# Attention outputs of a chunked recurrence: state rows and early v rows joined in one product, with a score buffer for each chunk

## The chip, the cores and the metric

One core of one Trainium2 chip. The metric is the device time of the program in microseconds, the median of the runs. The engines are named as the profile names them: PE is TensorE, DVE VectorE, ACT ScalarE, POOL GpSimd, and SP SyncE, which here only begins transfers.

## What is computed

The input x has 4 sequences of 1024 rows of 1024 numbers. Each row is normalised. From it come q, k and v (weights rounded to -1, 0 and 1 times a scale), 16 heads of 64, and a gate from a second linear layer. The attention is a recurrence over chunks of T = 128 rows, with a decay s for each head:

```python
def step(S, qkv_c):
    qi, ki, vi = qkv_c
    scores = jnp.einsum('bhtd,bhsd,hts->bhts', qi, ki, mask)     # mask: exp(-s (t - s')) for t >= s', else 0
    intra = jnp.einsum('bhts,bhsd->bhtd', scores, vi)
    cross = jnp.einsum('bhtd,ht,bhde->bhte', qi, lam_t, S)
    o = scale * (intra + cross)
    kv = jnp.einsum('bhtd,ht,bhte->bhde', ki, lam_rev, vi)
    return (lam_T * S + kv, o)
```

The outputs are normalised twice, projected, multiplied by the silu of the gate, and added to x.

## The kernel before

The rows are cut into 16 blocks (i = 0 to 15) of two chunks (c = 0 and 1), so 32 chunks g = 2i + c; eight chunks make a sequence, and the first chunk of one (g = 0, 8, 16, 24) has no state to read. Everything is held with channels on the partitions, two heads (e = 0, 1) of 64 on the 128 partitions of a pair r, eight pairs. Large products (q and k, v, the gate, the projection) run in float16 pieces against rounded weights; from block 2 on, v and the gate use seven products p1 to p7 of quarter size (Strassen's scheme), k from block 3 (`BY_TOKENS`) and the projection from block 4 to 14 (`BY_PRODUCTS`). Their sums of quarters are made by DVE.

There is no scheduler: each engine runs one written-out list of instructions in order, and semaphores hold them to each other. What matters around the change, in the order of a block:

- PE: q, the k products, projection products of the block before, the v products, then for chunk 0 the scores, v product p4, a gate product, a turn of k, the outputs (`outputs`, L938 and L942), the state update (L919); then the same for chunk 1 with gate products between. k product p4 (L839) waits for DVE's `add_k(i, 1)` (L1407), v product p4 (L813) for `add_v(i, 1)` (L1399).
- `outputs`: for each pair r, two f32 products state x decayed q (128 columns, L938) and two products v x masked scores (L942) into the same PSUM. The state of a pair is a 128 x 128 block whose off-diagonal quarters are zero.
- DVE: sums of quarters (L1378 and others), centring of the next block's rows (L1333, L1335), `decay_k_tokens` (L1532), `add_v`, `mask_scores` (L1523: scores in PSUM times the mask), `weight_o`, `add_state` (L1567).
- POOL: `add_out` (L2532), `norm_scale`, `decay_q` (L2481: q times its decay, two halves of 128 x 512 for a chunk), `decay_state` (L2493, two of 64 x 512), `bias_z` (L2466, L2468), `sum_squares`, `output_scale` (L2521, L2525), and in blocks 1 to 4 sums of weights. `decay_q(i, 0)` stands after `norm_scale(i + 1, ...)`; `decay_q(i, 1)` stands in `attention(i, 0)` after `bias_z`, since there is one buffer of decayed q, free after the outputs of chunk 0.
- SP: loads of x, stores of the output, and the turn of the row statistics through memory, in a written order.
- Masked scores and decayed q have one buffer each, in the tile `arena`; `scores_m` is shared in memory with `b_turned`, and with the row and pieces of the projection products.

Of the kernel before, what the change touches and what calls it, by code (L numbers as in the profile page):

```python
# [36 lines left out]
def program(nc, x, qkv_w, proj_w, decay, ffn_w, ffn_b, norm_cols, x_turned, out):  # L37
# [17 lines left out]
    with ExitStack() as ctx:  # L55
# [34 lines left out]
        QL_OFF = V_OFF + CHUNKS * C  # L90
        ST_OFF = QL_OFF + 2 * C
        SM_OFF = ST_OFF + 2 * PR * P
        ARENA = SM_OFF + H * T
# [4 lines left out]
        with nc.sbuf_tensor("arena", [P, ARENA], F32) as arena:  # L98
            pass
        sb("arena_low", [P, SM_OFF])  # L100

        o_row = sb("o_row", [P, CPH, T])
        o_split = sb("o_parts", [P, 3, 2, CPH, T], F16)
# [26 lines left out]
        v_tok = arena[:, V_OFF:QL_OFF].rearrange("p (c n) -> p c n", c=CHUNKS)  # L130
        q_decay = arena[:, QL_OFF:QL_OFF + C].rearrange("p (r t) -> p r t", r=PR)
        k_decay = arena[:, QL_OFF + C:QL_OFF + 2 * C]

        ow_first = k_decay.rearrange("p (r t) -> p r t", r=PR)
        state = arena[:, ST_OFF:SM_OFF].rearrange("p (k r e) -> p k r e", k=2, r=PR)
        scores_m = arena[:, SM_OFF:ARENA].rearrange("p (h e r t) -> p h e r t", h=HALF, e=2, r=CPH)

        b_turned = arena[:, SM_OFF:ARENA].rearrange("p (c j t) -> p c j t", c=CHUNKS, j=NCB)
# [7 lines left out]
        lam_T = sb("lam_T", [P, PR])  # L146
# [13 lines left out]
        diag = sb("diag", [P, CHUNKS, T])  # L160

# [36 lines left out]
        s_state0 = sem("state_zeroed")  # L198
# [138 lines left out]

        def passes_on(g):

            return g - g // NCHUNK  # L340
# [5 lines left out]
        def of_half(i, c, h):  # L346
            return chunk(i, c) * HALF + h + 1

# [347 lines left out]
        def tensor_program(pe):  # L696
# [514 lines left out]
        def vector_program(dve):  # L1211
# [297 lines left out]
            def mask_scores(i, c):  # L1509
# [8 lines left out]
                for half in range(HALF):  # L1518
                    dve.wait_ge(s_sc, HALF * g + half + 1)
                    if g > 0:  # L1520
                        dve.wait_ge(s_o, HALF * (g - 1) + half + 1)
# [1273 lines left out]
```

## Time and profile before

| | before |
|---|---|
| median of 3 runs (lowest to highest) | 1314.8 us (1313.32 to 1315.18) |
| span of the profiled execution | 1314.2 us |
| PE busy | 1289.1 us, 98% |
| DVE busy | 1008.4 us, 77% |
| ACT busy | 617.4 us, 47% |
| POOL busy | 600.4 us, 46% |
| granted TensorE clock | full in all 40 slices |
| moved by DMA | 90.3 MB, 69 GB/s over the span |

The profiled execution lasted 1314.2 us from its first to its last instruction, 0.6 us under the median of the timed runs. The page's busy times are averages over all stages; where a stage is bound by the hand-over from one engine to another is seen in the timelines of that stage. In a timeline, the columns are the start, the length (both in us), the engine, the line, the operation, the output and inputs, the shapes and the count of merged instructions, and in brackets the idle time before with what ended it. The length of several merged instructions runs from the start of the first to the end of the last; consecutive DVE instructions overlap by some 0.08 us.

### The profile page before, as it was taken

How to read it: one execution, taken by the hardware profiler on the slowest of the kernel's cores; microseconds unless marked ns; L12 is line 12 of the kernel's file. 1: busy time of each engine (PE TensorE's matmuls, PEld its weight loads, DVE VectorE, ACT ScalarE, POOL GpSimd, SP SyncE). 2: the span in 40 equal slices, each digit the busy share in tenths (PEclk: the TensorE clock that was granted, in tenths of full speed). 3: DMA queues.
4: the chain of work that ended last, by engine and by line, in shares of the span. 5: the costliest groups of instructions: out<-in, count | busy, mean ns of one | idle time of the engine just before them, and what ended most of it. 6: DMA issues, size and time to landing. Idle time of an engine off the chain costs nothing.

```text
span 1314.2 us, 25908 instructions
## 1 busy us (share of the span) xinstructions
PE 1289.1 (98%) x10263; PEld 824.8 (63%) x10263; DVE 1008.4 (77%) x1567; ACT 617.4 (47%) x1216; POOL 600.4 (46%) x537
## 2 busy tenths in 40 slices
PE   4999999999999999999999999999999999999998
PEld 2577767675665757566574656657566575756655
DVE  7888367687676887878788787877878788787755
ACT  5884144344434635446354544644436363544621
POOL 1442785955354435354432535435333443535352
PEclk9999999999999999999999999999999999999999
DMA  9631101203012030210303011030300304021020
GB/s 361 248 97 66 57 34 37 101 33 106 1 38 100 17 121 18 76 46 18 121 17 120 18 57 65 17 121 18 94 28 19 119 17 121 17 58 49 1 65 32
DMA packets 33433, 90.32 MB, mean 69 GB/s; under 512 B 10529, under 2 KB 10785, under 8 KB 33314
## 3 DMA queue, kind: packets, MB, share of 16 engines
q1 hardware_dynamic: 33024, 88.65, 20.0%
q8 instruction: 82, 1.34, 0.4%
q14 instruction: 37, 0.30, 0.1%
q10 hardware_dynamic: 290, 0.02, 0.0%
HBM read 71.85 MB, written 16.81 MB: 67 GB/s over the span
## 4 chain that ended last, share of the span: by engine, by line
PE 94%; DVE 2%; ACT 2%; DMA 1%; issue 1%; SPq 0%; POOL 0%; DVEq 0%; ACTq 0%; POOLq 0%
PE ring L854 20%; PE ring L787 13%; PE ring L813 13%; PE ring L839 12%; PE ring L1012 10%; PE ring L988 5%; PE att_ps L892 4%; PE att_ps L942 4%; PE att_ps L938 4%; PE ring L904 2%; PE att_ps L919 2%; PE ring L867 1%; PE ring L754 1%; DMA raw<-in_ffn_w 1%; ACT junk L1951 1%
## 5 line engine op out<-in xcount | busy, mean ns | idle before, releaser
L854 PE MATMUL ring<-b_lo,qkv_q 128*128 128x256 f16 x1216 | 268.2, 272 | 0.0
L854 PE MATMUL ring<-b_hi,qkv_q 128*128 128x256 f16 x1216 | 268.2, 273 | 0.0
L2532 POOL TENSOR_TENSOR xt<-xt,gate_even 128x512 f32<-128x512 f32 x58 | 90.6, 1564 | 172.5 <-DVE gate_even L1626 131.8
L854 PEld LDWEIGHTS ring<-b_hi,qkv_q 128*128 128x128 fp8e4 x1216 | 120.2, 99 | 15.8 <-issue 0.4
L854 PEld LDWEIGHTS ring<-b_lo,qkv_q 128*128 128x128 fp8e4 x1216 | 118.9, 98 | 15.6
L2506 POOL TENSOR_TENSOR sq<-sq,cols 128x1024 f32<-128x1024 f32 x29 | 55.0, 1896 | 126.8 <-DVE b_lo L1423 118.6
L2094 ACT ACTIVATE gate_even<-gate_even 128x512 f32<-128x512 f32 x60 | 37.3, 625 | 136.2 <-DVE gate_even L1454 136.1
L942 PE MATMUL att_ps<-arena 128*64 128x128 f32 x1024 | 95.0, 273 | 0.0
L938 PE MATMUL att_ps<-arena 128*64 128x128 f32 x896 | 88.5, 276 | 0.0
L1523 DVE TENSOR_TENSOR arena<-att_ps,mask 128x512 f32<-128x512 f32 x128 | 79.3, 680 | 11.0 <-PE att_ps L892 11.0
L2385 POOL TENSOR_TENSOR ln<-ln,small 128x3 f32<-128x3 f32 x32 | 37.4, 1168 | 100.2 <-DVE ln L1311 99.3
L2481 POOL TENSOR_TENSOR arena<-arena,lam_q 128x512 f32<-128x512 f32 x56 | 77.2, 1398 | 9.7 <-ACT arena L2110 7.0
L1454 DVE SCALAR_TENSOR_TENSOR gate_even<-ring,ln,gate_even 128x512 f32<-128x512 f32 x70 | 52.4, 748 | 29.0 <-PE ring L787 29.0
L2466 POOL TENSOR_TENSOR gate_even<-gate_even,bias 128x512 f32<-128x512 f32 x14 | 19.8, 1415 | 114.0 <-ACT gate_even L2070 113.9
L2110 ACT ACTIVATE arena<-ring,wscale 128x512 f32<-128x512 f32 x64 | 43.4, 679 | 58.0 <-PE ring L854 58.0
L892 PEld LDWEIGHTS att_ps<-arena 64*128 64x128 f32 x1024 | 59.7, 188 | 13.8 <-issue 13.8
L2493 POOL TENSOR_TENSOR arena<-arena,lam_T 64x512 f32<-64x512 f32 x48 | 61.6, 1283 | 13.5 <-DVE arena L1565 10.8
L892 PE MATMUL att_ps<-arena 64*128 64x128 f32 x1024 | 65.8, 278 | 0.5 <-ACT sq L2136 0.5
L1648 DVE SCALAR_TENSOR_TENSOR gate_even<-ring,wscale,gate_even 128x512 f32<-128x512 f32 x36 | 27.0, 749 | 50.7 <-PE ring L1012 36.2
L942 PEld LDWEIGHTS att_ps<-arena 128*64 128x64 f32 x1024 | 63.5, 137 | 0.7 <-issue 0.7
L2521 POOL TENSOR_TENSOR small<-small 128x1 f32<-128x1 f32 x32 | 18.5, 580 | 99.5 <-DVE small L1633 99.5
L787 PE MATMUL ring<-ffn_q,a_lo 128*128 128x512 fp8e4 x168 | 63.6, 379 | 0.0
(298 smaller groups left out, 3523.1 us busy)
## 6 DMA issues: line engine op xcount, KB each, us to landing
xt<-in_x SPq DMA_DIRECT2D x60, 512.0 KB, 3.7
out<-xt SPq DMA_DIRECT2D x31, 512.0 KB, 2.7
raw<-in_qkv_w SPq DMA_DIRECT2D x24, 512.0 KB, 15.8
y<-in_x_turned SPq DMA_DIRECT2D x14, 512.0 KB, 5.9
y_odd<-in_x_turned SPq DMA_DIRECT2D x14, 512.0 KB, 6.7
raw<-in_ffn_w SPq DMA_DIRECT2D x8, 512.0 KB, 9.8
norm_rows<-norm_out SPq DMA_DIRECT2D x14, 256.0 KB, 6.0
raw<-in_proj_w SPq DMA_DIRECT2D x6, 512.0 KB, 4.7
```

The lines of the kernel that those rows point to most:

```text
L787: ins = pe.matmul(ring[:, b, :], of[:, j, :], weights_of(weights)[:, j, :], start=(begins and j == 0 and k == 0), stop=(j == CPH - 1 and k ...
L813: ins = pe.matmul(ring[:, b, :], of[:, j, :], v_weights_of(weights)[:, j, :], start=(name in ("p1", "p5") and j == 0 and k == 0), stop=(j ...
L839: ins = pe.matmul(ring[:, b, :], of[:, j, :], k_weights_of(weights)[:, j, :], start=(name in ("p1", "p5") and j == 0 and k == 0), stop=(j ...
L854: ins = pe.matmul(ring[:, b, e * BT:(e + 1) * BT], qkv_q[:, cb, o:o + P], part[:, cb, :], start=(cb == 0 and part is b_hi and (e == 0 or i ...
L892: ins = pe.matmul(att_ps[:, 2 * half + e, j, :], k_t[rows, r, ts], q_t[rows, r, ts], start=True, stop=True)
L938: pe.matmul(att_ps[e * D:(e + 1) * D, half, j, :], state[:, passes_on(g) % 2, r, e * D:(e + 1) * D], q_decay[:, r, :], start=True, stop=Fa ...
L942: ins = pe.matmul(att_ps[e * D:(e + 1) * D, half, j, :], v_tok[:, c, r * P + e * D:r * P + (e + 1) * D], scores_m[:, half, e, j, :], start ...
L988: ins = pe.matmul(ring[:, b, :], part[:, cb, :], proj_q[:, cb, cs], start=(cb == 0 and k == 0), stop=(cb == NCB - 1 and k == 1))
L1012: ins = pe.matmul(ring[:, b, :], of[:, j, :], proj_weights_of(weights)[:, j, :], start=(name in ("p1", "p5") and j == 0 and k == 0), stop= ...
L1523: dve.tensor_tensor(scores_m[:, half, e, :, :], att_ps[:, 2 * half + e, :, :], mask[:, e, half * CPH:(half + 1) * CPH, :], ALU.mult).then_ ...
L2481: pool.tensor_tensor(q_decay[:, hs, :], q_t[:, hs, c * T:(c + 1) * T], lam_q[:, hs, :], ALU.mult).then_inc(s_ql, 1)
L2532: pool.tensor_tensor(o, o, gate_of(i)[:, c, cs], ALU.add).then_inc(s_add, 1)
```

## The change

For a non-first chunk, the first 64 tokens of the chunk (its keys) have scores with all 128 queries, the last 64 keys only with the last 64 queries, because of causality. The change uses that. For each chunk parity c there is a buffer `stacks[c]` with three sections of 64 query columns: section 0 holds (rows 0 to 63) the masked scores of the early keys with the early queries and (rows 64 to 127) decayed q of the early queries; section 2 holds zeros and decayed q of the late queries; section 1 holds the masked scores of all 128 keys with the late queries. `v_state` holds, for each head, 64 rows of v of the early keys above the 64 rows of the state. One joined product of v_state with sections 0 and 2 (128 columns) and one of v with section 1 (64 columns) replace two of 128 columns.

- `outputs`: the above; in first chunks one product of 128 columns as before. The waits for decayed q (both halves), the state, the copy of v and the zeros all stand ahead of half 0.
- `mask_scores`: four operations of 512 elements as before, cut by query half instead of head; it waits for the outputs of the same chunk a block ago.
- `decay_q`: two operations of 64 x 1024, one for each head half, from rows 0 to 63 or 64 to 127 to rows 64 to 127. `decay_q(i, 1)` moves from the middle of `attention(i, 0)` to right after `decay_q(i, 0)` (blocks 1 to 4) or after the last `add_out` of the block before (from block 5), ahead of `decay_state(i, 0)`; in block 0 it stays.
- `decay_state`: one operation of 64 x 1024. `add_state` writes both heads to rows 64 to 127.
- `copy_v`: the 64 early rows of v (256 KB) are copied by DMA into v_state; begun by SP at the end of each block's list for both chunks, by ACT for chunk 1 of block 0.
- `b_turned` moves so that it shares memory with the odd stack; some waits move with it. The host reserves less room for dynamic DMA.

```diff
@@ outputs
-                if not is_first(g):
-                    pe.wait_ge(s_ql, HALF * takes_over(g) + half + 1)
-                    if half == 0:
-                        pe.wait_ge(s_st, 2 * passes_on(g))
+                if not is_first(g) and half == 0:
+                    pe.wait_ge(s_ql, 2 * takes_over(g) + 2)
+                    pe.wait_ge(s_st, 2 * passes_on(g))
+                    pe.wait_ge(s_vcopy[c], copied(i, c))
+                    if takes_over(g) == 0:
+                        pe.wait_ge(s_zeros, CHUNKS)
...
                 for j in range(CPH):
                     r = half * CPH + j
-                    if not is_first(g):
+                    to = [att_ps[e * D:(e + 1) * D, half, j, :].rearrange("p (s t) -> p s t", s=2) for e in range(2)]
+                    v = [v_tok[:, c, r * P + e * D:r * P + (e + 1) * D] for e in range(2)]
+                    if is_first(g):
                         for e in range(2):
-                            pe.matmul(att_ps[e * D:(e + 1) * D, half, j, :],
-                                      state[:, passes_on(g) % 2, r, e * D:(e + 1) * D], q_decay[:, r, :],
-                                      start=True, stop=False, skip_group_check=True)
+                            ins = pe.matmul(to[e], v[e], stacks[c][:, 0:2, e, r, :], start=True, stop=True)
+                        continue
+
                     for e in range(2):
-                        ins = pe.matmul(att_ps[e * D:(e + 1) * D, half, j, :],
-                                        v_tok[:, c, r * P + e * D:r * P + (e + 1) * D],
-                                        scores_m[:, half, e, j, :], start=is_first(g), stop=True,
-                                        skip_group_check=True)
+                        pe.matmul(to[e], joined(g)[:, r, e, :], stacks[c][:, 0:3:2, e, r, :],
+                                  start=True, stop=False, skip_group_check=True)
+                    for e in range(2):
+                        ins = pe.matmul(to[e][:, 1, :], v[e], stacks[c][:, 1, e, r, :],
+                                        start=False, stop=True, skip_group_check=True)
@@ mask_scores
-                    if g > 0:
-                        dve.wait_ge(s_o, HALF * (g - 1) + half + 1)
-                    for e in range(2):
-                        dve.tensor_tensor(scores_m[:, half, e, :, :], att_ps[:, 2 * half + e, :, :],
-                                          mask[:, e, half * CPH:(half + 1) * CPH, :], ALU.mult).then_inc(s_scm, 1)
+                    if i > 0:
+                        dve.wait_ge(s_o, of_half(i - 1, c, half))
+                    for s, rows in enumerate((early, slice(0, P))):
+                        ts = slice(s * D, (s + 1) * D)
+                        dve.tensor_tensor(stacks[c][rows, s, :, hs, :], att_ps[rows, 2 * half:2 * half + 2, :, ts],
+                                          mask[rows, :, hs, ts], ALU.mult).then_inc(s_scm, 1)
@@ decay_q
-                pool.tensor_tensor(q_decay[:, hs, :], q_t[:, hs, c * T:(c + 1) * T], lam_q[:, hs, :],
-                                   ALU.mult).then_inc(s_ql, 1)
+                if i > 0:
+                    pool.wait_ge(s_o, of_half(i - 1, c, 1))
...
+                if c == 1 and i > 0 and by_products(i - 1):
+                    pool.wait_ge(s_ops, of_o_product(i - 1, "p3"))
+
+                    pool.wait_ge(s_add, of_out(i - 1, 0, 1))
...
+                for e in range(2):
+                    rows = slice(e * D, (e + 1) * D)
+                    q, by = (of.rearrange("p r (s t) -> p r s t", s=2)
+                             for of in (q_t[rows, :, c * T:(c + 1) * T], lam_q[rows, :, :]))
+                    pool.tensor_tensor(stacks[c][D:P, 0:3:2, e, :, :].rearrange("p s r t -> p r s t"), q, by, ALU.mult).then_inc(s_ql, 1)
+                    pool.wait_ge(s_ql, 2 * takes_over(g) + e + 1)
@@ decay_state
-                for e in range(2):
-                    rows, cs = slice(e * D, (e + 1) * D), slice(e * D, (e + 1) * D)
-                    pool.tensor_tensor(state[rows, (n + 1) % 2, :, cs], state[rows, n % 2, :, cs],
-                                       lam_T[rows, :].unsqueeze(2).to_broadcast([D, PR, D]), ALU.mult).then_inc(s_sd, 1)
-
-                    pool.wait_ge(s_sd, 2 * (n - g // NCHUNK - 1) + e + 1)
...
+                pool.tensor_tensor(to, of, lam_T[D:P, :].unsqueeze(2).to_broadcast([D, H, D]),
+                                   ALU.mult).then_inc(s_sd, 1)
@@ attention (POOL), c == 0
-                    decay_q(i, 1, 0)
-                    decay_q(i, 1, 1)
+                    if i == 0:
+                        decay_q(0, 1)
@@ the loop over blocks (POOL)
                     if by_products(i - 1):
-                        decay_q(i, 0, 0)
-                        decay_q(i, 0, 1)
+                        decay_q(i, 0)
                         add_out(i - 1, 1, 1)
                         add_out(i - 1, 1, 0)
                         add_out(i - 1, 0, 1)
+                        decay_q(i, 1)
...
-                        decay_q(i, 0, 0)
-                        decay_q(i, 0, 1)
+                        decay_q(i, 0)
+                        decay_q(i, 1)
@@ sync_program
+            def copy_v(i, c):
+
+                g = chunk(i, c)
+                if is_first(g):
+                    return
+                for by in v_at(i, c):
+                    sync.wait_ge(*by)
+                sync.wait_ge(s_o, HALF * (g - 1))
+                sync.dma_start(joined(g)[0:D, :, :, :].rearrange("p r e d -> p (r e d)"),
+                              v_tok[0:D, c, :]).then_inc(s_vcopy[c], DMA)
...
+                copy_v(i, 0)
+                copy_v(i, 1)
```

## Rows read from the trace of the kernel before

**Rows 1.** The page: the chain that ended last, share of the span by engine.
```profile
PE 94%; DVE 2%; ACT 2%; DMA 1%; issue 1%; SPq 0%; POOL 0%; DVEq 0%; ACTq 0%; POOLq 0%
```

**Rows 2.** Waits of PE: who for whom, us in total, times, longest us.
```profile
PE ring L813 <- DVE arena L1399: 1.6, 5, 0.3
```

**Rows 3.** Timeline of PE, block 9: outputs of chunk 0, state update, next product.
```profile
803.08 0.44 PE L938 MATMUL att_ps<-arena 128*64 128x128 f32 x4
...
806.63 1.10 PE L919 MATMUL att_ps<-arena,gate_odd 128*64 128x64 f32 x32
807.66 0.39 PE L787 MATMUL ring<-ffn_sum,sum_hi 128*128 128x512 fp8e4 x1
```

**Rows 4.** POOL's groups by line and shape: busy us, mean ns | idle before.
```profile
L2506 POOL TENSOR_TENSOR sq<-sq,cols 128x1024 f32<-128x1024 f32 x29 | 55.0, 1896 | 126.8 <-DVE b_lo L1423 118.6 <-ACT sq L2136 8.2
...
L2510 POOL TENSOR_TENSOR sq<-sq 128x512 f32<-128x512 f32 x29 | 36.8, 1271 | 2.3
L2510 POOL TENSOR_TENSOR sq<-sq 128x256 f32<-128x256 f32 x29 | 21.1, 729 | 2.3
```

**Rows 5.** Timeline of POOL, block 1: decay_state right after the outputs' scale.
```profile
189.50 2.15 POOL L2493 TENSOR_TENSOR arena<-arena,lam_T 64x512 f32<-64x512 f32 x2
```

**Rows 6.** Timeline, block 9: DVE's sums of quarters and POOL's decay_q beside them.
```profile
771.12 0.69 DVE L1378 TENSOR_TENSOR y_odd<-y_odd 128x512 f32<-128x512 f32 x1
...
771.82 1.26 POOL L2481 TENSOR_TENSOR arena<-arena,lam_q 128x512 f32<-128x512 f32 x1
...
771.85 1.78 DVE L1378 TENSOR_TENSOR y_odd<-y,y_odd 128x512 f32<-128x512 f32 x1
```

**Rows 7.** Timeline of DVE, block 9: the masks of chunk 1.
```profile
812.43 2.48 DVE L1523 TENSOR_TENSOR arena<-att_ps,mask 128x512 f32<-128x512 f32 x4 [0.35 <-PE att_ps L892]
```

**Rows 8.** Timeline, block 9: add_k(9, 1), k product p4, DVE's next wait.
```profile
780.51 0.74 DVE L1407 SCALAR_TENSOR_TENSOR gate_odd<-ring,wscale,gate_odd 128x512 f32<-128x512 f32 x1
...
781.85 0.38 PE L839 MATMUL ring<-k_sum_last,b_hi 128*128 128x512 fp8e4 x1
...
785.50 0.75 DVE L1648 SCALAR_TENSOR_TENSOR gate_even<-ring,wscale,gate_even 128x512 f32<-128x512 f32 x1 [2.87 <-PE ring L1012]
```

**Rows 9.** Timeline: decay_state to v product p4 in block 9; p4 in block 14.
```profile
793.25 3.48 POOL L2493 TENSOR_TENSOR arena<-arena,lam_T 64x512 f32<-64x512 f32 x2
...
794.30 2.98 DVE L1532 TENSOR_TENSOR gate_odd<-gate_odd,lam_k 128x512 f32<-128x512 f32 x2
...
797.20 1.40 DVE L1399 SCALAR_TENSOR_TENSOR arena<-ring,wscale,arena 128x512 f32<-128x512 f32 x2
...
798.65 0.39 PE L813 MATMUL ring<-v_sum_last,b_hi 128*128 128x512 fp8e4 x1
...
1190.43 0.39 PE L813 MATMUL ring<-v_sum_last,b_hi 128*128 128x512 fp8e4 x1 [0.33 <-DVE arena L1399]
```

**Rows 10.** Timeline, block 8: the second add_v and v product p4.
```profile
719.89 0.75 DVE L1399 SCALAR_TENSOR_TENSOR arena<-ring,wscale,arena 128x512 f32<-128x512 f32 x1 [0.39 <-PE ring L813]
...
721.77 0.39 PE L813 MATMUL ring<-v_sum_last,b_hi 128*128 128x512 fp8e4 x1
```

**Rows 11.** Timeline of PE, block 3: v product p4.
```profile
329.90 0.39 PE L813 MATMUL ring<-v_sum_last,b_hi 128*128 128x512 fp8e4 x1
```

**Rows 12.** Timeline of PE, block 1: the spread of the outputs' scale.
```profile
190.03 0.38 PE L973 MATMUL ring<-diag,mean_sq 128*128 128x128 f32 x1
```

**Rows 13.** Timeline, block 0: the masks of chunk 0, and its outputs.
```profile
98.81 2.47 DVE L1523 TENSOR_TENSOR arena<-att_ps,mask 128x512 f32<-128x512 f32 x4
...
100.41 0.76 PE L942 MATMUL att_ps<-arena 128*64 128x128 f32 x9
```

**Rows 14.** SP's last load in block 9 (timeline); DMA issues: count, KB, us to landing.
```profile
796.06 0.33 SPq L2673 DMA_DIRECT2D xt<-in_x  x1
...
out<-xt SPq DMA_DIRECT2D x1, 256.0 KB, 2.0
...
norm_rows<-norm_out SPq DMA_DIRECT2D x14, 256.0 KB, 6.0
```

More of the change, by code:

```diff
@@ L97, in program @@
             pass
[L98 to L103, printed above, removed]
+        arena = sb("arena", [P, ARENA])
         SQ = 2 * PR * T
@@ L197, in program @@
         s_ident, s_iota, s_cut = sem("ident_made"), sem("iotas_made"), sem("mask_cut")
-        s_state0 = sem("state_zeroed")
+        s_zeros = sem("stack_zeros_set")
+        s_vcopy = [sem(f"v_copied{c}") for c in range(CHUNKS)]
         s_ones, s_peak = sem("constants_set"), sem("peak_taken")
@@ L336, in is_last, with decays @@
             return g % NCHUNK == NCHUNK - 1
+        def decays(g):
+            return sum(not is_first(k) and not is_last(k) for k in range(g + 1))
         def passes_on(g):
@@ L347, in of_half, with copied, joined @@
             return chunk(i, c) * HALF + h + 1
+        def copied(i, c):
+            return DMA * sum(not is_first(chunk(k, c)) for k in range(i + 1))
+        def joined(g):
+            return v_state[:, passes_on(g) % 2, :, :, :]
         def of_ffn(i, c, h):
@@ L1559, in add_state @@
                 else:
-                    dve.wait_ge(s_sd, 2 * (passes_on(g) - (g // NCHUNK + 1)) + 2)
+                    dve.wait_ge(s_sd, decays(g))
                 for e in range(2):
-                    rows, cs = slice(e * D, (e + 1) * D), slice(e * D, (e + 1) * D)
-                    to = state[rows, (n + 1) % 2, :, cs]
+                    rows = slice(e * D, (e + 1) * D)
+                    to = v_state[D:P, (n + 1) % 2, :, e, :]
                     if is_first(g):
@@ L2468, in bias_z, with decay_q @@
                 pool.tensor_tensor(gate[:, 1, 0:BANK], gate[:, 1, 0:BANK], bias[:, 0:BANK], ALU.add).then_inc(s_zbias, 1)
-            def decay_q(i, c, half):
+            def decay_q(i, c):
                 g = chunk(i, c)
@@ L2490, in decay_state @@
                 pool.wait_ge(s_o, HALF * g)
-                for e in range(2):
-                    rows, cs = slice(e * D, (e + 1) * D), slice(e * D, (e + 1) * D)
-                    pool.tensor_tensor(state[rows, (n + 1) % 2, :, cs], state[rows, n % 2, :, cs],
-                                       lam_T[rows, :].unsqueeze(2).to_broadcast([D, PR, D]), ALU.mult).then_inc(s_sd, 1)
-                    pool.wait_ge(s_sd, 2 * (n - g // NCHUNK - 1) + e + 1)
+                if c == 1 and (by_products(i) or i == 1):
+                    pool.wait_ge(s_gamma, chunk(i, 0) + 1)
+                elif c == 1 and i > 1:
+                    pool.wait_ge(s_red, sums(chunk(i, 0)))
+                to, of = (v_state[D:P, k % 2, :, :, :].rearrange("p r e d -> p (r e) d") for k in (n + 1, n))
+                pool.tensor_tensor(to, of, lam_T[D:P, :].unsqueeze(2).to_broadcast([D, H, D]),
+                                   ALU.mult).then_inc(s_sd, 1)
+                pool.wait_ge(s_sd, decays(g))
             def sum_squares(i, c):
@@ L2605, in gpsimd_program @@
             pool.wait_ge(s_wout, w_n["qkv", QKV_TILES - 1])
-            pool.memset(state, 0.0).then_inc(s_state0, 1)
+            for stack in stacks:
+                pool.memset(stack[0:D, 2, :, :, :], 0.0).then_inc(s_zeros, 1)
             for i in range(NB):
@@ L2685, in load_turned, with copy_v @@
                 sync.dma_start(to, x_turned[row:row + P, :]).then_inc(s_xt[c], DMA)
+            def copy_v(i, c):
+                g = chunk(i, c)
+                if is_first(g):
+                    return
+                for by in v_at(i, c):
+                    sync.wait_ge(*by)
+                sync.wait_ge(s_o, HALF * (g - 1))
+                sync.dma_start(joined(g)[0:D, :, :, :].rearrange("p r e d -> p (r e d)"),
+                              v_tok[0:D, c, :]).then_inc(s_vcopy[c], DMA)
             def spread_norm(i):
```

65 lines of the change are left out of this document (44 added, 21 removed).

## Prediction

> **What bounds the kernel.** I read the page first: of the chain of work that ended last, 94% is TensorE (PE), in a span of 1314.2 us [rows 1]. PE is therefore the path: less PE work shortens the kernel, and any moment in which PE waits lengthens it. The second view is who waits for whom: PE waited for VectorE (DVE) in one place worth naming, the product at L813 behind the addition at L1399, five times and 1.6 us in all [rows 2]. The third is the timelines of PE, DVE and POOL in block 9, a typical one of the 16 blocks of 78.8 us. They show how much room stands between DVE and PE at the two places where DVE hands over work last. The granted clock is full throughout, so it is no term.
>
> **What PE saves.** In block 9 the outputs of chunk 0 start at 803.08 and the state update at 806.63, so the 64 instructions of the outputs (each f32 matmul is two) take 3.55 us, in groups of four 0.218 us apart, or 54.6 ns each. The update's 32 instructions have 64 columns and start at 806.63; the next product starts at 807.66. That is 1.03 us, of it some 0.15 the hand-over, so 28 ns each, or 32 with it [rows 3]. The change leaves 32 instructions of 128 columns (the joined products) and makes 32 of 64 columns: 32 x 54.6 + 32 x 28 = 2.64 us against 3.5, a gain of 0.86 us (0.72 at 32 ns). Outputs of the four first chunks keep their 128 columns. 28 chunks x 0.86 = 24 us; the bound below is 20.
>
> The Trainium skill (TensorE: Matmul & The Clock Gate, LDWEIGHTS) prices a weight load by its columns at P/1.2 ns, which as an estimate is 53 ns for 64 columns. If that set the pace, the short products would be no cheaper and the 24 us would be zero. The trace differs: such loads and matmuls follow each other in 28 to 32 ns [rows 3].
>
> **What POOL pays.** decay_q was two multiplications of 512 elements a partition and becomes two of 1024 on 64 partitions: the moves to other partitions are made half by half, and each half covers all eight pairs. POOL's time goes by elements a partition, not by partitions: two full f32 inputs cost 729 ns at 256 and 1271 at 512, a slope of 2.12 ns and so 2.35 us at 1024. With a broadcast input 1024 cost 1.90 us, and decay_state's 64 x 512 cost 1.03 undisturbed (2.15 for two, with the wait between them) [rows 4, 5]. I take 2.35 for the new operation, since both its inputs are full, with 1.9 as the bound below; nothing bounds it well above (the output goes to other partitions, in runs of 64), so 3.0 is my allowance. decay_state turns from 2 x 1.03 into one of 1.9: no term.
>
> By the Trainium skill (GPSIMD Engine Reference, Elementwise — side-by-side cycle accounting) 2048 elements take 4497 ns, so an estimate for 1024 is 2.25; every blocked operation below would be 0.1 us shorter and the sum some 3 us lower.
>
> **Why DVE pays for it too.** At 771.82 decay_q's first half starts, and DVE's subtraction of two SBUF tiles, 30 ns later, takes 1.78 us; the same operation without POOL beside it takes 0.69 [rows 6]. The DVE operation doesn't share, it runs when the POOL operation is over. Masking, which reads PSUM and one SBUF tile, is not held: four in 2.48 us while POOL sums squares [rows 7]. So masks (same count and elements), add_v and add_state keep their times, while sums, centring and decay_k_tokens stand behind POOL. What counts is the length of each POOL operation and what DVE owes PE afterwards.
>
> **Place A, the k products.** decay_q(i, 0) stays where it was, and each half holds DVE 2.35 - 1.27 = 1.08 us longer, 2.16 in all. DVE has no pause until add_k(i, 1) ends at 781.25; k product p4 waits for it and starts at 781.85 [rows 8]. A hand-over costs 0.06, so 0.54 is room. PE loses 2.16 - 0.54 = 1.6 us. DVE then waits for PE (2.87 us at 785.50 [rows 8]), so nothing is carried on.
>
> **Place B, the v products.** decay_q(i, 1), which stood behind the outputs of chunk 0 at 806.7, moves to before decay_state(i, 0), that is to 793.3. In the kernel before, the two halves of decay_state alternate there with the two decay_k_tokens of DVE (2.98 us for two that take 1.28 alone), then add_v twice, and v product p4 starts 0.06 us after them [rows 9]: no room. Now two operations of 2.35 stand in the place of two of 1.03: 2 x 1.32 = 2.6 us that PE waits. decay_state comes after them, at 799.5 to 801.4, before add_state at 807.8, and meets only masks. The wait for the last add_out is for POOL's own previous work; queued behind decay_q(i, 1) are decay_state and bias_z, whose input comes at 803.9: covered.
>
> A and B cost 4.3 us in blocks 5, 6, 7, 9, 10, 11, 13 and 14 (all eight have the same distances as block 9; of the last, block 14, the wait of p4 stands in [rows 9]): 34 us. Blocks 8 and 12 begin a sequence: no decay_q(i, 0), and no POOL work at B. There two operations come new, 4.7 less 0.2 by which the first runs under the centring; of these 4.5 us, add_v's pause of 0.39 and a room of 1.07 before p4 take 1.5 [rows 10]: 3.0 us each, 6.1.
>
> **The early blocks.** Block 3: a sum of weights on POOL has only one chunk's decays ahead of it, and p4 starts at 329.90 [rows 11]. From 316.7, the second half's start, POOL and DVE would alternate through three halves (7.05), decay_state (1.9), the sum (3.8) and DVE's four centrings (1.12 each), two decays (0.6) and two add_v (0.7): p4 at 336.2 to 336.5, and PE loses 6.3. Block 1: POOL's queue is full until it makes the outputs' scale, which is ready just ahead of decay_state at 189.50 and which PE takes at 190.03 [rows 5, 12]; four decays of +1.08 less 0.2 put it at 193.5, when PE, 1.3 us ahead, is ready at 188.8: 4.8. Block 0: the masks follow the rounding of weights without a pause and the second ends 0.3 before the outputs at 100.41 [rows 13]; decay_q, ahead of them, holds DVE 2.16 longer: 1.9. Blocks 4 and 15: 0.9 together (in 15 POOL has one sum of 3.83 already in that place).
>
> **The copies of v.** SyncE's last load of the block goes out at 796.06; v of chunk 0 is whole at 797.9, the outputs follow at 803.08, some 5 us, which B's stall doesn't shorten. A store of 256 KB lands in 2.0 us, norm_rows of the same size in 6.0 [rows 14]. I take 2.0 to 3, since the copy has 64 rows of 4 KB: hidden. At 6 it would cost 1 us in 12 blocks. Chunk 1's has 15 us of cover. After the two waits SyncE's next work is a load at the next block's start, so nothing queued behind them is late. PE's gathered waits (both halves of decay_q, the zeros, the copy) cost nothing by the same rows.
>
> **The sum.** -24 + 34.4 + 6.1 + 6.3 + 4.8 + 1.9 + 0.9 = +30.4 us. From the span of 1314.2 that is 1344.6; the measured median lies 0.6 above the span, so **1345 us**.
>
> **Rivals.**
> 1. *The operation is short* (1.9 us, as with a broadcast). A 0.7 and B 1.7 in eight blocks make 20; blocks 8 and 12, 4.2; the early ones 9: +9 net, 1324. For it: the linear rule is an extrapolation. Against: two slopes at 2.1.
> 2. *Faster: DVE isn't what PE waits for.* If at A and B DVE's operations win the port before the second halves, or the halves fall into pauses, only one of four delays remains; the stalls are under 20 us and PE's 24 decide: about 1300, at best 1291. It decides from an average delay of under 2 us a block. Against: at both places DVE has no pause and the trace alternates strictly.
> 3. *The operation is slow* (3.0 us, for the shifted partitions). Each delay grows by 0.65, A and B to 6.9: +61 us, 1376.
> 4. *The short products aren't shorter*: no 24 us, 1369. [rows 3] speak against it.
> 5. *The copy is late* (6 us or more behind other transfers): 12 us or more on top, 1357.
>
> **How the numbers follow.** The forecast has 0.60, rival 1 0.13, rival 2 0.13, rival 3 0.08, rivals 4 and 5 together 0.06. About 0.2% is what a measurement can tell from no change. Faster is 0.12 from rival 2; same 0.03 from its edge and that of rival 1; slower 0.85. The range, 1318 to 1364, reaches from under rival 1 to the forecast with operations of 2.7 us and leaves out most of rivals 2 and 3.
>
> **What would show it.** POOL's decay_q halves at 2.3 us; DVE's subtractions behind them at 2.8; decay_k_tokens two in 5.6; PE with new waits at L839 and L813 (k and v product p4) behind DVE of 1.6 and 2.6 us in each block, which the kernel before lacks; the outputs of a chunk in 2.7 us; no wait of PE for a DMA. I am wrong if PE's waits behind DVE add up to under 24 us, or if decay_q takes under 1.7.

## The result and the profile after

The changed kernel takes 1362.5 us (median of 4 runs, 1361.6 to 1362.9) against 1314.9 for the kernel before (1313.3 to 1315.2): ratio 1.0366, 95% interval 1.0351 to 1.0380. It is slower, by 47.6 us where 30 were forecast. The profiled execution spans 1361.5 us. Its page, with the columns of the page of before, has these lines: busy time by engine, the shares of the chain that ended last, and three groups of instructions.

```profile
PE 1286.5 (94%) x10263; PEld 807.4 (59%) x10263; DVE 1072.9 (79%) x1567; ACT 616.6 (45%) x1216; POOL 673.3 (49%) x514
...
PE 52%; DVE 24%; issue 11%; DMA 5%; POOL 5%; ACT 1%; SPq 0%; DVEq 0%; POOLq 0%; ACTq 0%
...
L2536 POOL TENSOR_TENSOR stack_odd<-arena,lam_q 64x1024 f32<-64x1024 f32 x32 | 88.4, 2763 | 3.7 <-POOL xt L2589 1.9
...
L1555 DVE TENSOR_TENSOR gate_odd<-gate_odd,lam_k 128x512 f32<-128x512 f32 x44 | 78.7, 1828 | 4.1 <-PE ring L919 4.1
```

The chain was 94% PE before [rows 1] and is 52% now; DVE has 24% of it. PE's busy time fell by 2.6 us only, although the outputs became shorter, and DVE's rose by 64.5 us with the same number of instructions: its decays of k take 1828 ns each, which is waiting counted as work. The waits say where PE stands. Columns: engine, tile, line, releaser: us in total, times, longest.

```profile
PE ring L828 <- DVE arena L1419: 32.7, 12, 5.9
...
PE ring L854 <- DVE gate_odd L1427: 9.3, 8, 1.2
PE att_ps L961 <- issue: 3.2, 1, 3.2
```

L828 is the v product and L1419 add_v: place B of the prediction; it was 1.6 us in five waits [rows 2]. L854 with L1427 is the k product behind add_k, place A. Block 9 of the changed kernel shows how B comes about. The timeline of DVE, POOL and PE (start, duration, engine, line, operation; in brackets the idle time before it and what ended it):

```profile
799.40 2.84 DVE L1382 TENSOR_TENSOR a_lo<-y,a_hi 128x512 f16<-128x512 f32 x1
802.37 2.62 DVE L1398 TENSOR_TENSOR y<-y_odd,y 128x512 f32<-128x512 f32 x1
...
822.58 5.59 DVE L1555 TENSOR_TENSOR gate_odd<-gate_odd,lam_k 128x512 f32<-128x512 f32 x2
828.09 1.40 DVE L1419 SCALAR_TENSOR_TENSOR arena<-ring,wscale,arena 128x512 f32<-128x512 f32 x2
...
821.74 5.88 POOL L2536 TENSOR_TENSOR stack_odd<-arena,lam_q 64x1024 f32<-64x1024 f32 x2 [0.17 <-POOL xt L2589]
...
829.54 0.43 PE L828 MATMUL ring<-v_sum_last,b_hi 128*128 128x512 fp8e4 x1 [2.53 <-DVE arena L1419]
829.77 0.63 PE L828 MATMUL ring<-v_sum_last,b_lo 128*128 128x512 fp8e4 x1
830.19 0.63 PE L828 MATMUL ring<-v_sum_last,b_hi 128*128 128x512 fp8e4 x1
...
832.32 0.63 PE L828 MATMUL ring<-v_sum_last,b_lo 128*128 128x512 fp8e4 x1
832.75 0.59 PE L802 MATMUL ring<-ffn_q,a_hi 128*128 128x512 fp8e4 x1
833.18 0.38 PE L802 MATMUL ring<-ffn_q,a_lo 128*128 128x512 fp8e4 x1
833.40 0.38 PE L802 MATMUL ring<-ffn_q,a_hi 128*128 128x512 fp8e4 x1
```

The reader sees two losses. The two decays of k take 5.59 us where they took 2.98 [rows 9], and PE stands for 2.53 us until add_v is done. That was forecast. Then the product itself runs with its matmuls 0.425 us apart, where they were 0.216 apart before, until 833.18. The windows of that stretch (window, its length, PE busy with its count, PEclk, share of the DMA engines, GB/s) name it:

```profile
827.00:829.50 2.50, 0.01 (x2) 1.00 0.09 34
829.50:833.00 3.50, 3.46 (x9) 0.54 0.35 75
833.00:835.00 2.00, 2.00 (x11) 0.96 0.13 29
```

The granted clock is 0.54 in the stretch behind the wait, that is, mostly at the lower of the two levels (1.2 GHz of 2.4), and PE had stood idle for 2.5 us when it fell. This second loss was in no term of the sum.

I lined up the starts of PE's matmul groups (same groups, same order) in both traces. The terms, predicted and measured, in us:

| term | predicted | measured |
|---|---|---|
| outputs, 28 chunks, with the hand-over behind | -24 | -22 |
| A, k product p4 (with 0.5 at v product p1 in block 5) | +13 | +11.1 |
| B, v product p4, eight blocks | +21.4 | +18.6 |
| blocks 8 and 12 | +6.1 | +6.0 |
| block 3 | +6.3 | +6.0 |
| block 1 | +4.8 | +5.2 |
| block 0 | +1.9 | +2.2 |
| blocks 4 and 15 | +0.9 | +0.8 |
| the fall of the clock behind B | 0 | +13.7 |
| waits of 0.4 to 0.6 for split_o and for the scale | 0 | +4 |
| pieces under 0.3 | 0 | +1.6 |
| sum | +30.4 | +47.2 |

### The profile page after: what moved, and what is told of

The parts are those of the page before. It is cut to its first block, busy times and chain, and to the rows that moved or that the text cites. A ratio compares the mean times of both kernels' runs of the same rounds, so it can differ in the third digit from the quotient of the medians.

```text
span 1361.5 us, 25949 instructions
## 1 busy us (share of the span) xinstructions
PE 1286.5 (94%) x10263; PEld 807.4 (59%) x10263; DVE 1072.9 (79%) x1567; ACT 616.6 (45%) x1216; POOL 673.3 (49%) x514
## 3 DMA queue, kind: packets, MB, share of 16 engines
q1 hardware_dynamic: 35184, 95.73, 21.4%
## 4 chain that ended last, share of the span: by engine, by line
PE 52%; DVE 24%; issue 11%; DMA 5%; POOL 5%; ACT 1%; SPq 0%; DVEq 0%; POOLq 0%; ACTq 0%
PE ring L869 14%; PE ring L802 12%; PE ring L828 4%; PE ring L1032 4%; PE ring L1008 3%; PE att_ps L961 3%; DVE a_lo L1382 3%; DMA norm_out<-norm_pair 3%; PE att_ps L907 2%; PE ring L854 2%; DMA y<-in_x_turned 2%; PE att_ps L934 2%; DVE y L1353 1%; DVE y L1398 1%; PE att_ps L964 1%
## 5 line engine op out<-in xcount | busy, mean ns | idle before, releaser
L2536 POOL TENSOR_TENSOR stack_odd<-arena,lam_q 64x1024 f32<-64x1024 f32 x32 | 88.4, 2763 | 3.7 <-POOL xt L2589 1.9
L1555 DVE TENSOR_TENSOR gate_odd<-gate_odd,lam_k 128x512 f32<-128x512 f32 x44 | 78.7, 1828 | 4.1 <-PE ring L919 4.1
L2057 ACT ACTIVATE arena<-ring,wscale 128x512 f32<-128x512 f32 x28 | 19.2, 687 | 117.8 <-PE ring L828 117.8
L2536 POOL TENSOR_TENSOR arena<-arena,lam_q 64x1024 f32<-64x1024 f32 x24 | 64.5, 2689 | 9.4 <-ACT arena L2147 6.6
L2147 ACT ACTIVATE arena<-ring,wscale 128x512 f32<-128x512 f32 x64 | 43.0, 679 | 49.6 <-PE ring L869 49.6
L802 PE MATMUL ring<-ffn_q,a_hi 128*128 128x512 fp8e4 x168 | 64.7, 385 | 0.0
L2567 POOL TENSOR_TENSOR sq<-sq 128x512 f32<-128x512 f32 (+1 forms) x58 | 58.1, 1001 | 4.6
L828 PE MATMUL ring<-v_sum_last,b_hi 128*128 128x512 fp8e4 x56 | 28.6, 510 | 32.8 <-DVE arena L1419 32.7
```

The source lines that it names most:

```text
L802: ins = pe.matmul(ring[:, b, :], of[:, j, :], weights_of(weights)[:, j, :], start=(begins and j == 0 and k == 0), stop=(j == CPH - 1 and k ...
L828: ins = pe.matmul(ring[:, b, :], of[:, j, :], v_weights_of(weights)[:, j, :], start=(name in ("p1", "p5") and j == 0 and k == 0), stop=(j ...
L1555: dve.tensor_tensor(k, k, lam_k[:, half * heads:(half + 1) * heads].unsqueeze(2).to_broadcast([P, heads, D]), ALU.mult).then_inc(s_kl, 1)
L2147: act.activation(q_t[:, r:r + 2, :], bank, ACT.Copy, scale=wscale[:, 7:8]).then_inc(s_q, 1)
L2536: pool.tensor_tensor(stacks[c][D:P, 0:3:2, e, :, :].rearrange("p s r t -> p r s t"), q, by, ALU.mult).then_inc(s_ql, 1)
L2567: pool.tensor_tensor(sq[:, 0, 0:m, :], sq[:, 0, 0:m, :], sq[:, 0, m:2 * m, :], ALU.add).then_inc(s_sqw, 1)
```

## The experiments

The kernel before was run beside every set, on the same chip: 1316.4 us beside e1 to e4, 1317.2 beside e5, e6, e9 and e10, 1314.6 beside e11 to e13. Expectations were written with the changed kernel at 1362.5; ratios are against the kernel before on the same chip.

**e1: decay_q(i, 1) behind add_v.**

```diff
@@ gpsimd_program, attention(i, 0), behind decay_state
+                    if i >= BY_TOKENS:
+                        pool.wait_ge(s_vsum, of_pair(i, 1))
+                        decay_q(i, 1)
@@ the loop over the blocks
-                        decay_q(i, 1)
@@
-                        decay_q(i, 1)
+                        if i < BY_TOKENS:
+                            decay_q(i, 1)
```

(decay_state(i, 0) also waits for POOL's own last add_out, which decay_q did for it.)

> Edit: from block 3 on the two operations of decay_q(i, 1) go behind decay_state(i, 0) and wait for add_v(i, 1), so that no POOL work of theirs stands beside the DVE work that v product p4 waits for. Everything else is the changed kernel (1362.5 us). Theory (DVE held by the two new operations at place B makes PE wait, and the fall of the granted clock follows that wait): the waits of v product p4 go (31.3 us in all in the changed kernel), and with them the products at half clock behind them (12.6 to 14 us): 1318 us, 1314 to 1324, granted clock 1.00 at v product p4. The wait of k product p4 (1.33 us in eight blocks) stays. Rival a (the clock falls for another reason, for instance the new shape of the outputs): 1331 us with the clock still at half behind v product p4. Rival b (PE waits at B for something else than POOL's place in the order, for instance for the copies of v): 1355 us or more.

Measured: 1316.4 us, ratio 1.0003 (0.9993 to 1.0013), mean granted clock 0.999. 46 us went at once: 33.6 from the steps to v product p4 and 12.6 from the product itself, whose matmuls are 0.217 us apart in every block. The theory holds, rivals a and b fall: outputs and copies are the same as in the changed kernel. Among its PE waits (first fence) and in DVE's timeline of block 9 (second):

```profile
PE ring L854 <- DVE gate_odd L1427: 9.3, 8, 1.2
```

```profile
799.10 2.99 DVE L1555 TENSOR_TENSOR gate_odd<-gate_odd,lam_k 128x512 f32<-128x512 f32 x2
802.01 1.40 DVE L1419 SCALAR_TENSOR_TENSOR arena<-ring,wscale,arena 128x512 f32<-128x512 f32 x2
```

No wait of L828 is left, the decays of k are back at 2.99, and place A stands untouched with its eight waits.

**e2: the operation shorter, nothing else.**

```diff
-                             for of in (q_t[rows, :, c * T:(c + 1) * T], lam_q[rows, :, :]))
+                             for of in (q_t[rows, :, c * T:(c + 1) * T],
+                                        lam_q[rows, :, 0:1].to_broadcast([D, PR, T])))
```

> Edit: the second input of decay_q is one column of lam_q spread over the tokens (another factor than the reference asks for), so each operation should take 1.90 us as the sum of squares with a broadcast does, not 2.34; order and waits are those of the changed kernel (1362.5 us). Theory (what DVE is held for is the length of the operation): two operations are 0.9 us shorter at each place, so k product p4 waits 0.4 instead of 1.33 in eight blocks (-7.5), v product p4 1.3 to 1.7 instead of 2.2 to 2.6 in eight and 2.1 instead of 3.0 in two (-9), block 3 and the early ones -3: 1343 us if the clock still falls behind the shorter wait, 1330 if it doesn't. Rival (the number of operations or the new outputs hold DVE, not their length): within 4 us of 1362.5.

Measured: 1333.4 us, ratio 1.0127 (1.0112 to 1.0142). Each operation is some 0.44 us shorter (POOL's mean in the group below fell from 2763 to 2326 ns; both include time held by DVE), and PE's steps shrank by 0.81 to 0.83 us at A and 0.86 to 0.88 at B, twice the 0.44. Two places gave less: 0.36 at A in block 5, where the wait of 0.5 at v product p1 went as well, and 0.46 at B in block 14.

```profile
L2536 POOL TENSOR_TENSOR stack_odd<-arena,lam_q 64x1024 f32<-64x1024 f32 x32 | 74.4, 2326 | 3.7 <-POOL xt L2589 1.9 <-POOL stack_odd L2664 0.2 <-POOL proj_sum_last L2498 0.2
```

And its PE waits:

```profile
PE ring L828 <- DVE arena L1419: 22.0, 11, 4.2
PE ring L854 <- DVE gate_odd L1427: 3.2, 8, 0.8
```

So PE pays for the length of the POOL operations, at most places one for one. The clock fell now only in blocks 3 and 8: 9.3 us of the 13.7 came back too.

**e3: the second pair of the outputs at 128 columns.**

```diff
-                        ins = pe.matmul(to[e][:, 1, :], v[e], stacks[c][:, 1, e, r, :],
+                        ins = pe.matmul(to[e], v[e], stacks[c][:, 0:2, e, r, :],
```

> Edit: the second pair of matmuls of the outputs has 128 columns again (it adds the early tokens' product a second time, so the output isn't the reference's); count and order of instructions and all POOL and DVE work are those of the changed kernel (1362.5 us). Theory (a 64-column matmul costs 28 us/1000 and a 128-column one 54.6, and PE is the path): 0.8 us more in each of 28 chunks, 1385 us, 1381 to 1388. Rival (the short products aren't cheaper, or the outputs stand beside other work): within 4 us of 1362.5.

Measured: 1376.9 us, ratio 1.0458 (1.0443 to 1.0474): 12 us above the changed kernel by the two ratios (0.0092 x 1316.4), where 23 were expected. The outputs did grow as forecast, by 0.82 us in each of the 28 chunks, 23 us in all. Between the two traces PE's last start moved by 14.8 us only. Two things took most of the rest off. The longer outputs covered short waits: those for the late copy in block 1, for split_o and for the outputs' scale shrank or went at nine places, 4.7 us in all. And the clock cost some 3 us less: the steps to v product p4 stayed as long (block 14's grew by 0.4), but the product behind ran at full clock in blocks 5, 11 and 13, where it had fallen, and fell in block 10, where it had not. The price of the columns is right; that a wait of the same length now costs the clock and now doesn't was the surprise that led to e10 and e11.

**e4: product p1 ahead of v product p4.**

```diff
                 if c == 0:
-                    v_product(i, "p4")
                     product(i, "p1")
+                    v_product(i, "p4")
```

> Edit: in attention_by_tokens(i, 0) PE issues product p1 of the feed-forward part ahead of v product p4, which waits for add_v(i, 1); POOL, DVE and ACT keep their orders; the rest is the changed kernel (1362.5 us). Product p1 takes 1.73 us and depends on nothing late, so the standstill ahead of v product p4 falls from 2.2 to 2.6 us to 0.5 to 0.9 in eight blocks, from 3.0 to 1.3 in two and from 6.0 to 4.3 in block 3. Theory (the granted clock falls only behind a longer standstill of PE): -19.6 us of waits and -11 of half clock, 1332 us, 1327 to 1337, with full clock at v product p4 but for block 3. Rival a (the clock falls at this place whatever PE waits): 1343 us, half clock still at the product behind the wait. Rival b (PE isn't held by v product p4's wait, another chain ends at the same time): above 1350.

Measured: 1337.9 us, ratio 1.0164 (1.0149 to 1.0179). The standstills fell as expected, to steps of 1.1 to 1.5 us, and full clock was granted behind each but block 3's 4.5. The 4 us that are missing are a new wait, which e13 shows again:

```profile
PE ring L828 <- DVE arena L1419: 11.9, 11, 4.1
...
PE ring L919 <- ACT arena L2057: 4.4, 13, 0.3
```

Turning k needs the ring bank of v product p4, which ScalarE empties; with p1 in front, that emptying is exposed (0.3 us of wait), and the outputs start 0.56 us late in 13 blocks. "Depends on nothing late" was true of p1 and not of what stands behind p4.

**e5: e1, and the second operation of decay_q(i, 0) behind add_k.**

```diff
                 for e in range(2):
+                    if e and c == 0 and i >= BY_TOKENS and by_products(i - 1):
+                        pool.wait_ge(s_ksum, of_k_pair(i, 1))
```

> Edit: the kernel of e1 (decay_q(i, 1) behind add_v; 1316.4 us), and in the blocks whose block before is done by products the second operation of decay_q(i, 0) waits for add_k(i, 1), so that only one operation of 2.35 us stands at place A where the kernel before had two of 1.27. Theory (DVE held at A makes k product p4 wait 1.33 us in blocks 5, 6, 7, 9, 10, 11, 13 and 14): those waits go, and the one of 0.5 in block 5: -11 us, 1305.3 us, 1303 to 1308. What could come new: the operation now runs from add_k's end beside the multiplication of the gate, the last add_out of POOL is 1 us later, and if that reached add_v again, place B would give back up to 1 us in nine blocks: 1315 (the rival, that the delay at A only moves on).

Measured: 1308.8 us, ratio 0.9939 (0.9925 to 0.9954): faster than the kernel before. By the two ratios that is 8.4 us less than e1, where 11 were expected. The eight steps to k product p4 fell by 1.33 us each and that of 0.5 went. What came new is small: 0.41 to 0.69 at v product p4 in eight blocks, 3.6 in all, since decay_state, one operation of 1.9, now holds DVE alone there and DVE arrives later. Place A is confirmed, and a part of its rival.

**e6: the late copy of block 1.**

```diff
@@ SyncE, end of the block
-                copy_v(i, 0)
+                if i > 1:
+                    copy_v(i, 0)
@@ ScalarE, block 1, behind v_out(1, 0, 1)
+                    copy_v(1, 0)
```

In the changed kernel's block 1 PE waits 3.21 us ahead of the outputs of chunk 0 for nothing that the profile names. SyncE's row shows the copy going out behind a load of 512 KB, and the DMA view from 174.9 on its landing time:

```profile
180.59 0.44 PE L961 MATMUL att_ps<-arena 128*64 128x128 f32 x4 [3.21 <-issue]
...
174.53 0.33 SPq L2731 DMA_DIRECT2D xt<-in_x  x1
174.96 0.54 SPq L2753 DMA_DIRECT2D arena<-arena  x1
```

```profile
arena<-arena SPq DMA_DIRECT2D x1, 256.0 KB, 5.4
```

174.96 + 5.4 = 180.4, and PE starts at 180.59.

> Edit: the copy of v of block 1, chunk 0 is begun by ScalarE behind its last v_out instead of by SyncE behind the load of 512 KB; all else is the changed kernel (1362.5 us on the first chip, 1364 by the ratio on this one). In the changed kernel the outputs of that chunk wait 3.3 us, up to the landing of the copy. Theory (POOL's full queue, which makes the outputs' scale, sets block 1, as in the forecast): the wait of 3.3 us goes from the outputs and comes back ahead of spread_gamma(1, 0); within 1 us of the changed kernel. Rival (the late copy is what block 1 loses): 3 us less, 1361.

Measured: 1363.4 us, ratio 1.0351 (1.0335 to 1.0366), against 1.0366 for the changed kernel: no difference. The 3.28 us ahead of the outputs went, and with them the fall of the clock behind that wait (a granted clock of 0.51 from 181.2 to 184.7 in the changed kernel); 4.88 came back ahead of spread_gamma(1, 0), in a wait of 5.47:

```profile
196.90 0.80 PE L993 MATMUL ring<-diag,mean_sq 128*128 128x128 f32 x2 [5.47 <-POOL diag L2583]
```

The copy was late, as rival 5 has it, but it isn't what block 1 loses: POOL's full queue sets that block, as in the forecast.

**e9: e5, e6 and the scale ahead of the last sum of v's weights.**

```diff
-                    sum_v_weights("T3")
                     output_scale(1, 0)
+                    sum_v_weights("T3")
```

(decay_state(1, 1) also waits for that sum.)

> Edit: e5 and e6 together, and in block 1 POOL makes the outputs' scale ahead of the last sum of v's weights (3.83 us) instead of behind it. Theory: of e5's 1305.3 us, block 1's waits go (2.5 at the outputs, 1.4 at spread_gamma): 1301.5 us, 1299 to 1305. Rival (the sum of weights or decay_state(1, 1), each 2 to 4 us later, is waited for in block 2): 1305 to 1308.

Measured: 1311.0 us, ratio 0.9956 (0.9941 to 0.9971), not better than e5. The waits at the outputs (3.2 us) went, and PE lost 3.4 at the projection behind block 1's state update, with 2.2 more of lower clock in it. Its trace shows why, at the timelines of DVE, POOL and PE:

```profile
193.83 4.70 DVE L1443 SCALAR_TENSOR_TENSOR b_lo<-y,cols,b_hi 128x128 f16<-128x128 f32 x4
198.46 1.21 DVE L1620 TENSOR_TENSOR o_lo<-ow,o_hi 128x1024 f16<-128x1024 f32 x1
...
192.12 3.83 POOL L2468 TENSOR_TENSOR qkv_q<-qkv_q 128x2048 fp8e4<-128x2048 fp8e4 x1
...
199.73 0.61 PE L1008 MATMUL ring<-proj_q,o_hi 128*128 128x512 fp8e4 x1 [4.72 <-DVE o_lo L1620]
```

The sum of weights now stands beside DVE's four operations at L1443, which take 4.70 us and 1.23 in e5, and split_o comes behind them. It is place B once more, at another line. Neither form of the rival named it: the late work was in block 1.

**e10: a standstill of PE in the kernel before, and nothing else.**

```diff
                 if c == 0:
+                    pe.wait_ge(s_scm, 4 * (chunk(i, 0) + 1))
                     v_product(i, "p4")
```

> Edit: the kernel before (1316.4 us on the last chip), with one more wait and nothing else: from block 3 on PE waits ahead of v product p4 until all four masks of chunk 0 are made. That is a standstill of some 2.4 us (four masks take 2.48) in 13 blocks with no change to POOL's, DVE's or ACT's work. Theory (the fall of the granted clock comes from PE's standstill and not from anything that POOL or the new outputs do): 31 us of waiting and, where the clock falls, 1.5 us for the products behind it; in the changed kernel it fell in five of eight blocks at 2.6 us and in e2 in one of three at 2.1, so in some half of the 13, 10 us: 1357 us, 1349 to 1368. Rival (the clock stays full without the change's own work): 1347 us and granted clock 1.000.

Measured: 1352.7 us, ratio 1.0266 (1.0249 to 1.0283). The trace is of the slowest of its four executions, 1357.1 us at a mean granted clock of 0.991; the others took 1350.6 to 1353.2 at 0.994 to 0.996. Its row of waits and v product p4 in blocks 6 and 11:

```profile
PE ring L813 <- DVE arena L1524: 32.3, 13, 3.7
```

```profile
576.46 0.61 PE L813 MATMUL ring<-v_sum_last,b_hi 128*128 128x512 fp8e4 x1 [3.68 <-DVE arena L1524]
576.86 0.63 PE L813 MATMUL ring<-v_sum_last,b_lo 128*128 128x512 fp8e4 x1
577.29 0.63 PE L813 MATMUL ring<-v_sum_last,b_hi 128*128 128x512 fp8e4 x1
...
986.12 0.39 PE L813 MATMUL ring<-v_sum_last,b_hi 128*128 128x512 fp8e4 x1 [2.71 <-DVE arena L1524]
986.34 0.38 PE L813 MATMUL ring<-v_sum_last,b_lo 128*128 128x512 fp8e4 x1
```

POOL, DVE and ScalarE do what they did in the kernel before, and the clock falls all the same, in blocks 5, 6, 7, 9, 13 and 14. The fall belongs to PE's standstill, not to the new outputs or to POOL. After 2.7 us it may also stay away, as in blocks 10 and 11.

**e11: a long standstill, in the kernel of e5.**

```diff
                 if c == 0:
+                    pe.wait_ge(s_ql, 2 * takes_over(chunk(i, 1)) + 2)
                     v_product(i, "p4")
```

> Edit: the kernel of e5 (1308.8 us, full clock at v product p4) with one more wait of PE: ahead of v product p4, from block 3 on, until both operations of decay_q(i, 1) are over, which start behind add_v(i, 1) and take 2 x 2.35 us. The step from the last matmul group of the scores to v product p4, 0.2 to 0.6 us in e5, 2.8 in the changed kernel, becomes 5.1 to 5.5 in 13 blocks: +62 us. Theory (the longer the standstill, the surer the fall of the clock; at 2.8 it fell in 5 or 6 of 8 blocks, at 6.2 in the one block that had it, at 1.9 or less in none): the clock falls in all 13 blocks and v product p4 and what follows take 1.5 to 1.7 us more each: +21, 1391 us. Rival (the fall depends on where a block lies and not on the standstill): it falls in about half of the blocks, 1381 us, and blocks 10 and 14 keep the full clock.

Measured: 1391.7 us, ratio 1.0586 (1.0565 to 1.0607), mean granted clock 0.973. Waits of 58.3 us in 13 places, up to 5.2; the clock fell in all 13, block 10 and 14 among them, and v product p4 and the product behind it took 28.0 us more than in e5. The rival falls. The rest of the table comes from all traces together: of each v product p4 from block 2 on, the step from the last start of the matmuls ahead of it to its own (0.2 us of it when nothing waits), and whether its matmuls stand over 0.23 us apart on average.

| step, us | places | clock fell |
|---|---|---|
| 0.2 to 0.6 | 95 | 0 |
| 0.7 to 2.0 | 26 | 0 |
| 2.3 to 2.6 | 5 | 1 |
| 2.8 to 3.0 | 30 | 18 |
| 3.2 | 6 | 5 |
| 3.8 to 6.2 | 20 | 20 |

**e12: e5, with decay_state(i, 0) behind add_v too.**

```diff
                 if c == 0 and i > 0 and by_products(i - 1):
                     pool.wait_ge(s_add, of_out(i - 1, 0, 1))
+                    pool.wait_ge(s_vsum, of_pair(i, 1))
```

> Edit: the kernel of e5 (1308.8 us), and decay_state(i, 0) too waits for add_v(i, 1) where POOL's add_out stands ahead of it. In e5 the step to v product p4 is 0.61 us in eight blocks where it is 0.2 elsewhere, since DVE's decays of k stand behind decay_state. Theory: that 0.4 us goes in eight or nine blocks, -3.5 us: 1305 us. Rival (POOL's queue behind add_v, decay_state 1.9 and decay_q 4.7, ends at 805.2 instead of 803.3 in the times of block 9 of the kernel before, and holds the decays of k of chunk 1 and bias_z, so that the outputs' weights and the state come late): 1312 us or more.

Measured: 1307.7 us, ratio 0.9947 (0.9932 to 0.9961). The steps to v product p4 are 0.20 us in every block from 3 on; 3.65 us went there and 1.4 came at one output of block 13, which waits 1.3 us for POOL's decay_q, in the queue that the rival named. Against e5's 0.9939 it can't be told apart, so the forecast 3.5 us less isn't shown by the times. Its first PE waits, of the whole span:

```profile
PE ring L750 <- DVE y L1343: 12.5, 2, 11.8
PE att_ps L961 <- issue: 3.3, 1, 3.3
PE ring L1008 <- DVE o_lo L1620: 2.4, 3, 1.4
```

L828 and L854 are gone from the list.

**e13: e5 with product p1 first.** The edit is that of e4.

> Edit: the kernel of e5 (1308.8 us) with product p1 ahead of v product p4, as in e4. Theory (the 0.4 us by which PE waits for add_v in eight blocks is filled by product p1, and nothing of v product p4's comes late, since outputs need chunk 0's v and masks alone there): -3.5 us, 1305 us. Rival (the first outputs then wait for the masks instead, as they did in e4 for 0.56 us): within 1 us of 1308.8.

Measured: 1312.6 us, ratio 0.9984 (0.9974 to 0.9993), slower than e5. The 0.4 us went, and the 0.56 ahead of the outputs came in 13 blocks, as in e4, behind the second half of turning k; block 13 lost 1.7 more there. By the two ratios it is 5.9 us above e5, where the theory had 3.5 less and the rival within 1. My rival had the place right and the cause and the size wrong: it is ScalarE's emptying of the bank, not the masks.

## Why the prediction was right, and where it fell short

**The mechanism held.** The sign, both places and the reason were as written: PE pays at A and B for the length of decay_q's operations, because DVE's operations with two SBUF inputs are held for them. e1 takes away the place and e2 the length, and each removes what the theory says. The Trainium skill (SBUF — State Buffer, "Who interferes with whom") describes such a shared port between VectorE and GpSimd; the trace agrees, with two decays of k in 5.59 us beside POOL and 1.28 without it.

**Operation length.** 2.35 us was forecast; where nothing holds them, the operations take 2.34 to 2.35 us (in the trace of e12, 2.34 at 781.63).

**The outputs.** Forecast 0.86 us a chunk, measured 0.82 with the hand-over; e3 gives the same 0.82 back. Rival 4 is refuted.

**Place A**: 1.6 forecast, 1.33 measured. DVE was delayed by 1.93 us (2.84 + 2.62 against 1.78 + 1.75), not by 2.16; 1.33 of it reached PE, so that the room was 0.6, about the 0.54 that I had.

**Place B**: 2.6 us was forecast on top of "no room". PE's wait is in fact 2.6 us in all eight blocks, but in blocks 6, 7, 10, 11 and 14 there had been one of 0.4 already. Those are the five waits of [rows 2]; I had read them and not subtracted them. So the term is 18.6, not 21.4. Blocks 8, 12, 3, 0 and 1 came within 0.4 us of their terms; in block 1 the sum was right although the wait that one sees first is another (e6).

**The copies.** They land in 2.8 us (median of 27), inside the 2.0 to 3 forecast, and no output but that of block 1 waits for one.

**The step that failed** stands in the first part: "The granted clock is full throughout, so it is no term." It was full because, between 200 and 1300 us, PE's waits in that trace were five of at most 0.3 us [rows 2]; my own sum put standstills of 2.6 to 6.3 us there, and the clock was not asked again. That left out 13.7 of the 17 us that are missing. The trace of before shows what the lower clock costs, but no fall. The same eight instructions of L735 and the first large product, from PE's timeline:

```profile
11.71 1.97 PE L735 MATMUL ring<-ident,y 128*128 128x128 f32 x8 [11.71 <-DVE y L1323]
...
26.45 0.63 PE L754 MATMUL ring<-ffn_q,a_lo 128*128 128x512 fp8e4 x1
26.87 0.63 PE L754 MATMUL ring<-ffn_q,a_hi 128*128 128x512 fp8e4 x1
...
30.18 0.38 PE L754 MATMUL ring<-ffn_q,a_hi 128*128 128x512 fp8e4 x1
30.40 0.38 PE L754 MATMUL ring<-ffn_q,a_lo 128*128 128x512 fp8e4 x1
...
38.38 1.04 PE L735 MATMUL ring<-ident,y 128*128 128x128 f32 x8
```

L735 takes 1.97 us at 11.71 and 1.04 at 38.38, and the product's starts are 0.43 us apart to 29.9 and 0.22 from 30.2 on. So PE worked at half pace from its first instruction until 30 us and no full pace stands ahead of it, although the page has full clock in all 40 slices; the pace of equal matmuls is the surer sign. The stretch from 26.06 cost 1.9 us (half of 3.8). With that for each of the eleven standstills of 2.6 us or more in my sum it would have been 51, an estimate; in fact the clock fell at eight of them, for 1.7 to 1.9 us each. The other 4 us are short waits for split_o and the outputs' scale in blocks 1, 2, 3, 7, 8, 11 and 12, for which I had no rows.

**How near it was.** 1362.5 lies inside the range, 1318 to 1364, by 1.5 us. The upper end stood for operations of 2.7 us; they took 2.34, and what filled the room was the clock and the short waits, of which the range knew nothing; the 2.8 us too much at B made up for as much of them. That the time is in the range is luck in this respect; the sign, the places and the terms of A, blocks 8 and 12, block 3 and the outputs are not.

What stays open: why a standstill of 2.8 to 3.0 us costs the clock in 18 places and not in 12. In the changed kernel and in e6 it was the same five of the eight blocks, in e3 and e10 others, so it isn't the block. The program alone doesn't decide it either: e10's four executions, with the same program on the same chip, differ in the mean granted clock (0.991, 0.996, 0.995 and 0.994) and by 6.5 us in time. No run here isolates what does.

## What to carry to other kernels

A POOL operation with SBUF inputs can cost DVE its whole length where DVE's own operation reads two tiles of SBUF, so ask of each one what DVE owes to the bounding engine right behind it; moving two operations behind one addition was worth 46 us here, twice what the matmuls saved. When a sum puts new standstills on PE, price the clock behind each as well: here 1.3 to 2.9 us for each fall, most often 1.7, on top of the wait. And before a wait at a semaphore is called the cost, take it away alone, as in e6: in a block that another queue sets, it only moves.

## What the runs showed of the hardware

That the granted clock falls behind a single standstill of 2.5 us, in a program whose PE is busy to 98% without it, was not expected, nor that it is not certain there: 0 of 26 at steps of 0.7 to 2.0 us, 18 of 30 at 2.8 to 3.0, 20 of 20 from 3.8 on. Once fallen it stayed so for 2.7 to 6.0 us of PE's work, most often 3.0 to 3.4, and what runs there takes twice its time (matmuls 0.425 us apart against 0.216).

The length of the POOL operation doesn't depend on the shift of 64 partitions or on writing in runs of 64: 2.34 us at 1024 elements lies on the line through 256 and 512 of [rows 4], which gives 2.35.
